# Causal mask of the attention maxima: 26 rows of steps in the q and k stacks in place of an identity product with a mask

## What is computed

```python
w = einsum('bhqd,bhkd->bhqk', q, k) / sqrt(16)
if causal_bool:             # self: key <= query
    w = where(tril(ones), w, neg)
if tril_diag2_additive:     # cross: key <= query + 2
    w = w + where(tril(ones, k=2) == 0, neg, 0)
if extra_bias is not None:  # cross: a logit per key
    w = w + extra_bias[:, None, None, :]
a = einsum('bhqk,bhkd->bhqd', softmax(w), v)
```

## Time and profile before

| what | value |
|---|---|
| median of 3 runs | 1208.4 us (1208.26 to 1210.92) |
| the profiled execution | 1205.04 us, span 1203.3 us |
| mean granted TensorE clock | 0.977 of 2.4 GHz |
| TensorE, VectorE, ScalarE, GpSimd busy | 91%, 66%, 51%, 37% |
| TensorE on the chain that ended last | 67% |
| first S matmul | 74.57 us from the span's start |

### The profile page before, as it was taken

How to read it: one execution, slowest core, us unless ns; L and a number is a source line. 1 busy time by engine, 2 the same in 40 slices (tenths; PEclk the granted TensorE clock), 3 DMA queues, 4 the chain that set the end, 5 groups by cost and what they waited for, 6 DMA issues and landing times.

```text
span 1203.3 us, 20614 instructions
## 1 busy us (share of the span) xinstructions
PE 1089.1 (91%) x7360; PEld 654.3 (54%) x7360; DVE 792.5 (66%) x1898; ACT 612.3 (51%) x1154; POOL 441.2 (37%) x805
## 2 busy tenths in 40 slices
PE   5659889899999999999999999999899999898877
PEld 2335546464556545674466645675466645464444
DVE  3448667777866777667876777767876677565223
ACT  1126455556644565545654575545744465455413
POOL 3204443435443523435343433435442342324220
PEclk9769999999999999999999999999999999999989
DMA  8951256271434535262254526253354412400000
GB/s 234 137 91 29 50 79 101 43 98 28 68 53 68 71 56 87 37 89 45 48 72 63 76 38 90 50 72 50 57 76 63 58 28 49 59 14 2 9 9 18
DMA packets 53528, 74.16 MB, mean 62 GB/s; under 512 B 9571, under 2 KB 27939, under 8 KB 53412
## 3 DMA queue, kind: packets, MB, share of 16 engines
q1 hardware_dynamic: 53428, 72.86, 39.1%
HBM read 17.45 MB, written 4.19 MB: 18 GB/s over the span
## 4 chain that ended last, share of the span: by engine, by line
PE 67%; DVE 12%; ACT 8%; issue 5%; DMA 4%; SPq 4%; POOL 2%; DVEq 0%; ACTq 0%; POOLq 0%
PE dense L536 16%; PE dense L530 14%; PE pv_out L608 11%; PE scores L594 8%; PE max_scores L574 8%; DVE row_max L810 4%; PE max_scores L577 3%; PE dense L524 3%; SPq L501 3%; DMA q_stack<-parts_q 2%; ACT inner L725 2%; ACT probs L699 1%; DMA q_stack<-max_rows 1%; PE dense L631 1%; DVE rest_k L843 1%
## 5 line engine op out<-in xcount | busy, mean ns | idle before, releaser
L699 ACT ACTIVATE probs<-scores 128x512 f32<-128x512 f32 (+3 forms) x768 | 383.4, 529 | 338.0 <-PE scores L594 334.0
L810 DVE TENSOR_REDUCE row_max<-max_scores 128x1 f32<-128x512 f32 (+6 forms) x1024 | 443.8, 481 | 138.7 <-PE max_scores L577 137.2
L968 POOL TENSOR_SCALAR_AFFINE_SELECT probs<-probs 128x256 f32<-128x256 f32 x512 | 215.6, 440 | 513.2 <-ACT probs L699 513.0
L574 PE MATMUL max_scores<-k_stack,q_stack 96*128 96x512 bf16 (+7 forms) x1024 | 284.5, 304 | 19.1 <-DVE row_max L810 15.1
L594 PE MATMUL scores<-q_stack,k_stack 98*128 98x512 bf16 (+7 forms) x1024 | 266.3, 301 | 32.8 <-ACT probs L699 17.7
L608 PE MATMUL pv_out<-probs,v_ones 128*32 128x512 f32 (+6 forms) x2048 | 166.5, 442 | 0.0
L574 PEld LDWEIGHTS max_scores<-k_stack,q_stack 96*128 96x128 bf16 (+1 forms) x1024 | 100.4, 98 | 95.5 <-issue 45.2
L594 PEld LDWEIGHTS scores<-q_stack,k_stack 98*128 98x128 bf16 (+1 forms) x1024 | 89.5, 98 | 97.4 <-ACT probs L699 28.7
L536 PE MATMUL dense<-mlp_w,inner 128*128 128x256 f32 x512 | 122.3, 385 | 9.4 <-DVE rest_k L843 4.2
L530 PE MATMUL dense<-feat_b,fc_w 128*128 128x512 f32 x256 | 125.0, 615 | 2.5 <-ACT rest_k L734 1.1
L536 PEld LDWEIGHTS dense<-mlp_w,inner 128*128 128x128 f32 x512 | 94.1, 190 | 29.3 <-DVE rest_k L843 5.4
(11 more groups left out here) (87 smaller groups left out, 1251.2 us busy)
## 6 DMA issues: line engine op xcount, KB each, us to landing
q_stack<-parts_q SPq DMA_DIRECT2D x192, 128.0 KB, 4.9
k_stack<-parts_k SPq DMA_DIRECT2D x192, 128.0 KB, 5.3
x_in<-in_x SPq DMA_DIRECT2D x8, 512.0 KB, 8.4
x_in<-in_ctx SPq DMA_DIRECT2D x8, 512.0 KB, 8.0
hidden<-in_x SPq DMA_DIRECT2D x8, 512.0 KB, 6.3
out_y<-hidden SPq DMA_DIRECT2D x32, 128.0 KB, 1.7
fc_w<-in_w_fc SPq DMA_DIRECT2D x1, 1024.0 KB, 10.1
mlp_w<-in_w_mlp SPq DMA_DIRECT2D x1, 1024.0 KB, 14.7
```

The source lines that it names most:

```text
L574: pe.matmul(max_scores[:, bank, c0:c0 + W[q]], queries[0:rows_, head, q * P:(q + 1) * P], keys[0:rows_, head, 0:W[q]], start=True, stop=False)
L699: nc.scalar.activation(probs[:, head % (2 * GH), c0:c0 + w], scores[:, part % EXP_BANKS, 0:w], ACT.Exp, scale=SCALE).then_inc(exp_done, 1)
L810: last = nc.vector.tensor_reduce(row_max[:, g % 2, c:c + 1], max_scores[:, part % MAX_BANKS, c0:c0 + W[q]], AX.X, ALU.max)
L968: nc.gpsimd.affine_select(out=v, in_=v, compare_op=ALU.is_ge, fill=0.0, base=q0 - kb * P + LAST[at.kind], pattern=[[0, 2], [1, P]], channe ...
```

## The change

The mask product goes, with the tiles `mask_self`, `mask_cross` and their memsets and selects. The q and k stacks get 26 rows more (`KALL` to `KSTEP`, 101 to 127). In q they hold, for the query at place p of its block, a step value; in k large negative values for the keys behind it, so that the product of these rows is a large negative number for masked pairs and nothing for the others. M now uses two matmuls for each query block but the first: one without the steps on the keys before the diagonal block (99 rows), one with all 127 rows on the diagonal block. All attentions have the same rows: self attentions have a bias of 0 (`no_bias`). Since M's second matmul runs over the rows of the maxima too, a transfer sets these to 0 ahead of each q load (`no_max`).

The new rows are written by `constant_rows`, for turn 0 before the first item, for turn 1 behind the stack loads of batch 0, and the loads of proj2, fc and mlp weights move behind them. GpSimd makes the steps with ten selects, each of which waits for the one before.

```diff
-KMAX = {"self": STACK, "cross": STACK + 3}
-KALL = {kind: KMAX[kind] + 2 for kind in KMAX}
+KMAX = STACK + 3
+KALL = KMAX + 2
+STEP = 5
+STEPS = -(-(P - 1) // STEP)
+KSTEP = KALL + STEPS
+STEP_Q = [2.0 ** (50 - 25 * i) for i in range(STEP)]
+STEP_K = [-2.0 ** (25 * j - 52) for j in range(1, STEP + 1)]
+LOADS = {"q": 7, "k": 6}
...
+        def mask_from(kind, q):
+            return 0 if q == 0 else P * q + LAST[kind]
...
-            for dst, src in ((proj1_w, w_proj1), (kv2_w, w_kv2), (q2_w, w_q2), (proj2_w, w_proj2),
-                             (fc_w, w_fc), (mlp_w, w_mlp)):
...
+            load((proj1_w, w_proj1), (kv2_w, w_kv2), (q2_w, w_q2))
+            def constant_rows(turn_):
                 for half in range(2):
-                    sp.dma_start(k_stack[turn_][half][KMAX["self"]:KALL["self"], :, :],
-                                 signs["minus"][0:2, :].unsqueeze(1).to_broadcast([2, NH // 2, T])
-                                 ).then_inc(const_rows_loaded, 16)
+                    queries, keys = q_stack[turn_][half], k_stack[turn_][half]
+                    for dst, src in ((queries[STACK:KMAX, :, :], signs["plus"][:]), (keys[STACK:KMAX, :, :], no_bias),
+                                     (keys[KMAX:KALL, :, :], signs["minus"][0:2, :]),
+                                     (queries[KALL:KSTEP, :, :], step_q),
+                                     (keys[KALL:KSTEP, :, :], step_k[:, LAST["cross"]:LAST["cross"] + T])):
+                        sp.dma_start(dst, src.unsqueeze(1).to_broadcast([src.shape[0], NH // 2, T])
+                                     ).then_inc(const_rows_loaded[turn_], 16)
...
             def rows_for_cross(n):
...
                     if n == 2:
-                        for dst, src in ((keys[KMAX["cross"]:KALL["cross"], :, :], signs["minus"][0:2, :]),
-                                         (queries[STACK:KMAX["cross"], :, :], signs["plus"][:])):
-                            sp.dma_start(dst, src.unsqueeze(1).to_broadcast([src.shape[0], NH // 2, T])
-                                         ).then_inc(cross_rows_loaded, 16)
...
+                        sp.dma_start(keys[KALL:KSTEP, :, :], step_k[:, 0:T].unsqueeze(1).to_broadcast([STEPS, NH // 2, T])
+                                     ).then_inc(cross_rows_loaded, 16)
                     elif n == 2 * NB - 1:
-                        sp.dma_start(keys[STACK:KALL["cross"], :, :], k_stack[0][half][STACK:KALL["cross"], :, :]
+                        sp.dma_start(keys[STACK:KSTEP, :, :], k_stack[0][half][STACK:KSTEP, :, :]
                                      ).then_inc(cross_rows_loaded, 16)
-                        sp.dma_start(queries[STACK:KMAX["cross"], :, :], q_stack[0][half][STACK:KMAX["cross"], :, :]
-                                     ).then_inc(cross_rows_loaded, 16)
+            sp.wait_ge(consts_pool, POOL_CONSTS)
+            constant_rows(0)
...
+                            if name[0] == "q" and ready is hi:
+                                sp.dma_start(dst[KMAX:KALL, :, :].rearrange("r h (t p) -> r (h t) p", p=P),
+                                             no_max[:].unsqueeze(1).to_broadcast([2, NH // 2 * TB, P])
+                                             ).then_inc(stack_loaded[name][part], 16)
...
+                        if n == 0 and name == "k1" and part == 1:
+                            constant_rows(1)
+                            load((proj2_w, w_proj2), (fc_w, w_fc), (mlp_w, w_mlp))
...
                         for q in MAX_TILES[r]:
-                            pe.matmul(max_scores[:, bank, c0:c0 + W[q]],
-                                      queries[0:rows_, head, q * P:(q + 1) * P],
-                                      keys[0:rows_, head, 0:W[q]], start=True, stop=False)
-                            last = pe.matmul(max_scores[:, bank, c0 + q * P:c0 + W[q]], ident_b[:],
-                                             mask_of(at.kind, q), start=False, stop=True)
+                            m0 = mask_from(at.kind, q)
+                            if m0 > 0:
+                                pe.matmul(max_scores[:, bank, c0:c0 + m0],
+                                          queries[0:KMAX, head, q * P:(q + 1) * P],
+                                          keys[0:KMAX, head, 0:m0], start=True, stop=True)
+                            last = pe.matmul(max_scores[:, bank, c0 + m0:c0 + W[q]],
+                                             queries[0:KSTEP, head, q * P:(q + 1) * P],
+                                             keys[0:KSTEP, head, m0:W[q]], start=True, stop=True)
                             c0 += W[q]
...
-            for kind in mask:
-                nc.gpsimd.memset(mask[kind][:], 0.0).then_inc(consts_pool, 1)
+            for zero in (no_max[:], no_bias, step_q, step_k):
+                nc.gpsimd.memset(zero, 0.0).then_inc(consts_pool, 1)
...
-            for kind in mask:
-                nc.gpsimd.affine_select(out=mask[kind][:], in_=mask[kind][:], compare_op=ALU.is_ge, fill=NEG,
...
+            for n, fill in enumerate(STEP_Q):
+                v = step_q.rearrange("p (t q) -> p t q", q=P)
+                pool.wait_ge(consts_pool, 9 + n)
+                nc.gpsimd.affine_select(out=v, in_=v, compare_op=ALU.not_equal, fill=fill, base=-n,
+                                        pattern=[[0, TB], [1, P]], channel_multiplier=-STEP).then_inc(consts_pool, 1)
+            for n, fill in enumerate([STEP_K[-1]] + STEP_K[:-1]):
+                v = step_k[:, LAST["cross"]:].rearrange("p (t k) -> p t k", k=P)
+                pool.wait_ge(consts_pool, 9 + STEP + n)
...
```

More of the change, by code:

```diff
@@ L281, in block_kernel @@
         ident_b = sb("ident_b", [P, P], BF16)
-        mask = {"self": sb("mask_self", [P, P], BF16), "cross": sb("mask_cross", [P, P + 2], BF16)}
+        no_max = sb("no_max", [2, P], BF16)
         minus_half = sb("minus_half", [P, TB])
@@ L307, in block_kernel @@
         gelu_temp.append(gelu_temp[0])
-        q_stack = [[sb(f"q_stack_{k}{h}", [KALL["cross"], NH // 2, T], BF16) for h in range(2)] for k in range(2)]
-        k_stack = [[sb(f"k_stack_{k}{h}", [KALL["cross"], NH // 2, T], BF16) for h in range(2)] for k in range(2)]
+        q_stack = [[sb(f"q_stack_{k}{h}", [KSTEP, NH // 2, T], BF16) for h in range(2)] for k in range(2)]
+        k_stack = [[sb(f"k_stack_{k}{h}", [KSTEP, NH // 2, T], BF16) for h in range(2)] for k in range(2)]
         v_ones = [sb(f"v_ones_{k}", [P, TB, VROW]) for k in range(2)]
@@ L332, in block_kernel @@
         consts_dve = sem("consts_dve")
-        const_rows_loaded = sem("const_rows_loaded")
+        const_rows_loaded = [sem(f"const_rows_loaded_{turn_}") for turn_ in range(2)]
         cross_rows_loaded = sem("cross_rows_loaded")
```

42 lines of the change are left out of this document (21 added, 21 removed).

## The result

The changed kernel took 1233.5 us (median of 4 runs, 1228.75 to 1235.68) against 1208.3 for the kernel before (4 runs): a ratio of 1.020 (95% interval 1.016 to 1.024). It is longer, well clear of the noise; whether by more or less than 2% the interval leaves open. Measured again beside the experiments it was 1231.9 us and 1.019 (1.017 to 1.022).

The account below looks back on a forecast made before the run. TensorE was taken to bound the middle, the DMA engines the startup up to 75 us. Terms -34 + 21.5 + 10.4 + 1.2 = -0.9 us gave 1207.5 us, no change; 8-in-10 range 1188 to 1227.

Parts of the forecast that it names:

- The matmuls, -34: TensorE: 1,024 mask products removed, less the cost of splitting query blocks, shorten the kernel by 34 us (bounds -25 to -57).
- I take nine tenths: Matmul term: of 37 us left on the chain nine tenths come through, as VectorE's work comes in lumps; -34 us.
- the sign was 57: Check on TensorE: with line 577 gone its busy time should fall by about 57 us.
- Rival 5: Matmul saving: VectorE takes over a third of it, -25 instead of -34, 1216.5 us, slower; chance 0.08.
- The splits, put at 0 to 4 us: TensorE: 768 more matmuls on the same columns, each with a weight load, cost 0 to 4 us; 2.3 taken.
- Startup, +21.5: Before the first S: constants, weights, turn 1 rows and no_max delay it by 21.5 us (17 to 27), to near 96 us.
- +8.3 forecast: Startup: GpSimd's ten dependent selects delay the statistics and everything behind them, up to the first stack load, by 8.3 us.
- 6.6 + 5.2 = 11.8: Startup DMA queue: moved proj2, fc and mlp weights cost 6.6 us, constant rows of turn 1 5.2, ahead of first max_rows.
- Mostly absorbed while the other 14 engines set the pace: Startup: no_max transfers ahead of four q loads, 0.5 us each, are mostly hidden; with SP's issue time +1.4 us.
- The tail, +10.4: Last cross attention: 31-row copies on one DMA engine, 62 packets at 0.31 us, delay the maxima and S by 10.4 us.
- rival 3: Tail: long copies run against the stack loads' ports, maxima 22 us later, 1229 us; decides from 0.38 us a packet; chance 0.15.
- Small waits, +1.2: Two waits for q stacks on the chain: one more issue of 0.6 us ahead of each, +1.2 us (0 to 3).

Follow-up runs that it names:

- the spread version: The late version with the later weights and turn 1's constant rows spread over the first three groups of max_rows: 1197.9 us, ratio 0.988.
- 29 + 2: Changed kernel with the 31-row copy ahead of the last attention issued as copies of 29 and 2 rows, a control: 1229.2 us, ratio 1.017.
- 16 + 15: Changed kernel with the 31-row copy ahead of the last attention issued as copies of 16 and 15 rows: 1213.0 us, ratio 1.003.
- the late version: Changed kernel, tail copy cut 16 and 15, proj2/fc/mlp weights and turn 1 rows behind first max_rows, engines waiting for identity only: 1201.8 us, 0.996.

## Why the prediction was wrong

It said no change, 1207.5 us; the kernel is 25 us slower. Three terms of the sum were mis-sized, all in the same direction, and the range ended at 1227 below the result. By the two spans the change is +23.7 where the sum had -0.9. Of the 24.6 us between them the matmuls and small waits make 14.4 (-18.4 measured outside the startup and the stall, -32.8 forecast), the startup 5.7 and the tail 4.6. So the largest error is in the share of the saving that gets through, which the forecast named, beside the tail copy, as the place where it was most easily wrong.

- *The matmuls, -34.* The step that failed is "I take nine tenths" of the 37 us on the chain (which is 33.3; the text has 34). With the mask products simply gone the kernel is 26 us shorter by the medians, 21.6 by the spans. TensorE also had less to lose than was said: its busy time fell by 37.6 us (42.1 with the mask products simply gone) where the sign was 57, and by 6.1 us per batch in the middle, of which 3.6 came through. Rival 5 (-25, "VectorE takes over a third") had the size; its mechanism is not shown, since halving ScalarE's work returns as much as halving VectorE's. The stretch from the first S to the second hidden load gained nothing at all. Here it is of before and of the kernel without mask products; TensorE has 1.8 us less of busy time in it, and the mean granted clock is down from 0.96 to 0.93:

```profile
74.57:191.40 116.83, 104.88 (x776) 60.33 (x780) 79.94 (x212) 62.92 (x123) 46.18 (x90) 0.96 0.31 50
```

```profile
76.39:193.31 116.92, 103.10 (x655) 52.74 (x655) 81.14 (x213) 62.32 (x124) 46.95 (x92) 0.93 0.32 52
```

  That the lower clock is the reason was not tried by itself. The splits, put at 0 to 4 us, cost no time that shows, and the middle with 127 contraction rows is as long as with 96 and 99, as said.
- *Startup, +21.5; measured +27.15.* That the miss is no larger is luck: the constants were put 2.9 us too high and the rest 8.5 us too low. The constants were too dear: +8.3 forecast, 5.4 measured, as the selects follow each other without the gap that was added, and the path behind them had some slack. What was moved or added ahead of the first max_rows was too cheap. Weights and rows of turn 1 were to cost 6.6 + 5.2 = 11.8; taken out of the way (the spread version) the first S comes 18.5 us earlier, 101.72 to 83.23, of which up to 1.4 may be the engines' earlier start behind the identity (first no_max at 25.30 in place of 26.73). What remains against before, 83.23 - 74.57 - 5.4 = 3.2 with 2 us of scatter, is left for the rows of turn 0 and no_max, of which the forecast had 1.4, the rows of turn 0 at nothing. The step that failed is pricing bytes at a rate and adding them up: SP's own issues stretch (8.61 us for one), what is issued behind them is late as a whole, and moving one of the two early brought 3.7 or 4.3 us, both 3.5. "Mostly absorbed while the other 14 engines set the pace" failed as well: the last 4 us ran on two engines. What loads these two stays open; moving the six small copies and changing the shape of the max_rows transfer did not take it away. A candidate that no run left out is no_max itself. The forecast had 0.5 us on each of the two engines for each of its four transfers, 2 us, from the 16 ns of a packet where little else ran. By the packet records of the trace their 256 packets of 256 B took 10.5 us ahead of the first max_rows, 41 ns each, which is 5.3 us for each engine if two carry them, as the forecast had it.
- *The tail, +10.4; measured +15.0 up to the S that waits, 16.2 in the whole (against 29 + 2).* The mechanism, one engine for 31 rows and the maxima behind them, was right and is shown by 16 + 15 against 29 + 2. The term was mis-sized by the pace of the packets beside other transfers: 62 at 0.31 us each were to take 19.2 us. By the packet records of the trace they ran from 1004.7 to 1029.0 us, 24.3 us. The first 27 took 0.50 us each, while the k loads and the hidden load ran on the other engines; the 35 from 1018 us on took 0.31 each, as forecast (25 GB/s). So rival 3, which was to decide from 0.38 us a packet on, came true in part: 0.39 on average. Behind them came 24 packets of 2 KB, 32 of 1 KB and the maxima, 3.7 us, as forecast. Behind the stall little is lost: the granted clock stays at 0.50 for another 4.4 us, and from the S that waited to the end the changed kernel takes 193.8 us, against 192.7 with the copy cut in 16 and 15.
- *Small waits, +1.2*: nothing to see in the middle, which is as long as without any of it.

## What to carry to other kernels

Before a copy between SBUF tiles grows, look at its row count: 31 rows cost 15 us of stall that 16 + 15 rows do not. What waits need not be what the copy is for: here half of the maxima of the attention before stood behind it. Work that is moved "out of the way" in a saturated queue goes behind the transfer that the path waits for, and in portions: with both loads in front and early the first S came at 98.2 us, with both behind at 85.8 and 83.2. And the share of the chain is no estimate of what its removal returns where the other engines take over in many short waits: leave the work out of the old kernel first, and read the ceiling (26 us by the medians here) before paying for it.

## What was not expected of the hardware

Issuing is not free when much is queued: the load of in_ctx took 8.61 us to issue in the changed kernel, 11.83 with the rows early, both right behind the weights, and 0.58 in the late version, where only stack loads stood in front. At the tail the same shows for the maxima: their one transfer took 10.17 us to issue behind the copies of 31 rows, 0.70 with the copies cut in 16 and 15. A transfer of max_rows in two single rows is no faster than one of two rows (first S 102.14 against 101.70 us), and the two kernels with it are 4.7 and 6.7 us slower by their medians; why was not settled.
